# Routing products in another PSUM bank, and the last band's sums ahead of the maps' combination

## The reference

```python
x_proj = einsum('bchw,oc->bohw', x, proj_w)               # 128 -> 64 channels
att1 = _route(x_proj, att1_w, att1_b, [w3, w5], [b3, b5], 1)          # depthwise, 3x3 or 5x5
att2 = _route(att1, att2_w, att2_b, [w7, w9, w11], [b7, b9, b11], 3)  # depthwise, dilation 3
out = concatenate([att1, att2], axis=1)
att = concatenate([out.mean(1), out.max(1)], axis=1)      # two maps per sample
att = sigmoid(conv2d(att, sp_w, pad 3) + sp_b)            # 7x7, 2 -> 2
gate = att[:, 0:1] + att[:, 1:2]
return out * gate + x

def _route(x, att_w, att_b, conv_ws, conv_bs, dilation):
    pooled = x.mean(axis=(2, 3))
    idx = argmax(softmax(pooled @ att_w.T + att_b, axis=1), axis=1)   # which kernel this sample takes
    return the depthwise convolution of x with kernel idx
```

## Time and profile before

| | |
|---|---|
| median of three runs | 6009.83 us |
| profiled execution | 6016.42 us |
| span from first to last instruction in it | 6014.7 us |
| TensorE matmul busy | 4768.7 us (79%) |
| VectorE busy | 3136.8 us (52%) |
| ScalarE busy | 2827.8 us (47%) |
| GpSimd busy | 1039.5 us (17%) |
| DMA | mean 214 GB/s |

### The profile page before, as it was taken

One profiled execution on the slowest core, in us unless ns is written; L12 is line 12 of the kernel. 1 busy time (PEld: TensorE's weight loads), 2 busy tenths in 40 slices (PEclk: granted clock), 3 DMA queues, 4 the chain that ended last, 5 costly groups with the idle time before them and its releaser, 6 DMA issues.

```text
span 6014.7 us, 156600 instructions
## 1 busy us (share of the span) xinstructions
PE 4768.7 (79%) x62816; PEld 3244.4 (54%) x62816; DVE 3136.8 (52%) x3931; ACT 2827.8 (47%) x5378; POOL 1039.5 (17%) x1574
## 2 busy tenths in 40 slices
PE   5678887888878888887888888788888878885453
PEld 2336474655647465564746547474654747464453
DVE  3315455554645546474554547455464755545345
ACT  3455554544545454454545454454545445451120
POOL 2001011111112111121211111121111212111232
PEclk8889999988989989898999989899998989897675
DMA  9655787979888797988879788897978888796957
GB/s 241 185 159 172 173 209 226 230 219 224 237 210 218 216 233 218 222 244 209 218 219 235 216 222 244 200 227 213 237 219 222 246 202 224 211 213 176 221 135 198
DMA packets 1033176, 1284.58 MB, mean 214 GB/s; under 512 B 670749, under 2 KB 865736, under 8 KB 1001885
## 3 DMA queue, kind: packets, MB, share of 16 engines
q1 hardware_dynamic: 899468, 723.43, 50.5%
q0 software_dynamic: 64304, 410.01, 21.8%
q10 hardware_dynamic: 69026, 146.11, 9.5%
HBM read 950.16 MB, written 456.70 MB: 234 GB/s over the span
## 4 chain that ended last, share of the span: by engine, by line
PE 50%; DMA 21%; SPq 9%; DVE 8%; issue 7%; ACT 3%; ACTq 1%; POOL 1%; another core or an unknown queue 0%; DVEq 0%; POOLq 0%
PE psC L1086 19%; PE psA L1022 10%; PE psA L1023 9%; DMA RX<-w_d 6%; SPq L439 6%; DMA RX<-in_x_dram 5%; PE psB L1054 3%; PE psA L958 3%; PE psB L1065 2%; PE psB L1032 2%; DMA out_dram<-RX 2%; DMA RX<-nat_d 2%; DVE L L1375 2%; PE psB L967 2%; DMA map_d<-RX 2%
## 5 line engine op out<-in xcount | busy, mean ns | idle before, releaser
L1086 PE MATMUL psC<-RX 61*60 61x96 f32 (+7 forms) x49152 | 1479.9, 268 | 276.1 <-POOL RX L680 129.4
L1086 PEld LDWEIGHTS psC<-RX 61*60 61x60 f32 x49152 | 1412.8, 134 | 341.9 <-issue 329.2
L875 ACT ACTIVATE L<-psC 124x120 f32 (+4 forms) x2048 | 396.8, 287 | 885.6 <-PE psC L1086 830.5
L1022 PE MATMUL psA<-X,RX 128*128 128x240 f32 x1280 | 638.0, 588 | 129.7 <-ACT RX L840 128.2
L680 POOL COPY RX<-RX 64x720 f32<-64x720 f32 x512 | 426.2, 839 | 1408.8 <-DMA RX<-w_d 1407.5
L845 ACT ACTIVATE X<-psA,bias 128x246 f32<-128x246 f32 x1024 | 626.6, 722 | 56.2 <-issue 25.6
L1054 PE MATMUL psB<-ident,L 124*128 124x124 f32 x2160 | 381.1, 318 | 334.9 <-DVE RX L1395 163.7
L1310 DVE TENSOR_REDUCE MM<-L 124x135 f32<-124x2160 f32 (+1 forms) x192 | 535.3, 2844 | 212.7 <-ACT L L875 212.7
L1395 DVE TENSOR_TENSOR RX<-psB,RX 128x360 f32<-128x360 f32 (+7 forms) x1200 | 359.2, 350 | 546.5 <-PE psB L1054 485.6
L1023 PE MATMUL psA<-X,RX 128*128 128x240 f32 x1280 | 632.5, 583 | 0.0
L865 ACT ACTIVATE RX<-L 128x1080 f32 (+1 forms) x256 | 542.4, 2127 | 147.8 <-DMA L<-strip_d 147.7
(11 more groups left out here) (122 smaller groups left out, 5008.2 us busy)
## 6 DMA issues: line engine op xcount, KB each, us to landing
RX<-in_x_dram POOLq DMA_DIRECT2D x48, 2560.0 KB, 15.2
RX<-w_d ACTq DMA_DIRECT2D x512, 180.0 KB, 4.4
RX<-in_x_dram SPq DMA_DIRECT2D x128, 720.0 KB, 9.1
out_dram<-RX SPq DMA_DIRECT2D x128, 720.0 KB, 8.4
nat_d<-X SPq DMA_DIRECT2D x320, 280.0 KB
L<-strip_d SPq DMA_DIRECT2D x192, 405.0 KB, 10.5
strip_d<-nat_d SPq DMA_DIRECT2D x48, 1440.0 KB
RX<-nat_d POOLq DMA_DIRECT2D x130, 400.0 KB, 5.1
```

Of the source, the lines that this page charges most:

```text
L875: ins = nc.scalar.activation(dst[:, 0:NU2 - par, 15 * r:15 * r + nq, par, :], src[:, par:BR:2, :, :], ACT.Identity)
L1022: nc.tensor.matmul(o[:, :, 0:T1], w[:, ch, 96:224], rhs, start=True, stop=False, skip_group_check=True)
L1086: ins = nc.tensor.matmul(o[:, :, 0:kk, a:b], w2t[2 * q + p][rows, ch, z:z + PB], src[rows, 2 * p + ch, 0:nf, 3 * cg + dc:3 * cg + dc + kk, ...
```

## The change

The product of the sums (L1002) leaves `route` and becomes `route_stats`, which TensorE runs before the last fill's transposes. It and the three logits products write columns 400 to 451 of psC[3], which nothing else uses, in place of psA[0]; so the wait for ScalarE's last copy out of psA goes. VectorE reads them there. On VectorE, `combine` moves from before `take_x` of band 5 to behind `route_means` and stands ahead of `route_indices`.

```diff
                     if f == MAPS_AFTER and t.two:
                         turn_map2(t.m)
+                route_stats(s)
                 turn_x(s, *fills[-1])
+
+            def route_stats(s):
+                if isinstance(s, int) and s == 0:
+                    pe.wait_ge(psum_set, 1)
+                wait_alone(pe, stats_ready, s + 1)
+                nc.tensor.matmul(psC[3][0:C2, 400:425], projt[:, :], stats[:, :, :].rearrange("p r c -> p (r c)"),
+                                 start=True, stop=True).then_inc(stats_mm, 1)
 
             def route(t):
                 s = t.s
-                pe.wait_ge(stats_ready, s + 1)
-                wait_alone(pe, xc_ready, NFS * (s + 1))
-                nc.tensor.matmul(psA[0][0:C2, 0:25], projt[:, :], stats[:, :, :].rearrange("p r c -> p (r c)"),
-                                 start=True, stop=True).then_inc(stats_mm, 1)
                 if t.two:
                     wait_alone(pe, proj_evac, NFS * (s + 1))
                     spatial(t.m, 0)
                 wait_alone(pe, pool_ready, s + 1)
-                for n, (o, m, rhs) in enumerate(((32, 2, a1t), (40, 3, a2t), (48, 3, a2t))):
-                    ins = nc.tensor.matmul(psA[0][0:1, o:o + m], pooled[:, n:n + 1], rhs[:, :], start=True, stop=True)
+                for n, (o, m, rhs) in enumerate(((432, 2, a1t), (440, 3, a2t), (448, 3, a2t))):
+                    ins = nc.tensor.matmul(psC[3][0:1, o:o + m], pooled[:, n:n + 1], rhs[:, :], start=True, stop=True)
...
-                step(nc.vector.tensor_copy(psx[:, :, :].rearrange("p r c -> p (r c)"), psA[0][0:C2, 0:25]))
+                step(nc.vector.tensor_copy(psx[:, :, :].rearrange("p r c -> p (r c)"), psC[3][0:C2, 400:425]))
...
                     for b in range(2, NB1 - 1):
                         take_x(s, b)
-                if t.two:
-                    combine(m)
                 if t.new:
                     take_x(s, NB1 - 1)
                     stats_total(s)
                     route_means(s)
+                if t.two:
+                    combine(m)
+                if t.new:
                     route_indices(s)
```

More of the change, by code:

```diff
@@ L1255, in route_indices @@
                 dve.wait_ge(logits_mm, s + 1)
-                step(nc.vector.tensor_tensor(lg[:, 0:2], psA[0][0:1, 32:34], attb[:, 0:2], ALU.add))
-                step(nc.vector.tensor_tensor(lg[:, 2:5], psA[0][0:1, 40:43], attb[:, 2:5], ALU.add))
-                step(nc.vector.tensor_tensor(lg[:, 5:8], psA[0][0:1, 48:51], attb[:, 2:5], ALU.add))
+                step(nc.vector.tensor_tensor(lg[:, 0:2], psC[3][0:1, 432:434], attb[:, 0:2], ALU.add))
+                step(nc.vector.tensor_tensor(lg[:, 2:5], psC[3][0:1, 440:443], attb[:, 2:5], ALU.add))
+                step(nc.vector.tensor_tensor(lg[:, 5:8], psC[3][0:1, 448:451], attb[:, 2:5], ALU.add))
                 l2 = lg[:, 2:8].rearrange("p (v k) -> p v k", k=3)
```

## The result

The changed kernel took **6091.28 us** as the median of four runs (6084.23 to 6111.00) against 6000.84 us for the kernel before in the same session. The ratio is 1.0158, with a 95% interval of 1.0124 to 1.0191: 1.6% slower. Its profiled execution took 6084.23 us, of which 6082.5 us are the span; the forecast made against the profiled execution was 6083.5.

The account below looks back on a forecast made before the run. No engine bounds the kernel for long; each turn is a chain of hand-overs. 47.7 (order) + 20.2 (clock) - 0.8 = +67.1 us on the median 6009.83 gives 6077 us, 1.1% slower; range 6030 to 6105.

Parts of the forecast that it names:

- What sets the first convolution's start: Start of each turn: the two halves of the 7x7 convolution set the first convolution's start, not the routing.
- Rivals A: Absorbed: later in the turn, the later start costs nothing or only part; 6043 half absorbed, 6010 wholly; chance 0.14.
- B: Faster: the longer quiet stretch lets output-phase loads land sooner; 5999 with one load regained, 5920 with two; chance 0.06.
- Sums of band 5: VectorE, ahead of the maps: sums take 4.5 us from 2009.6, ready near 2014.1, 3.5 us before the product.
- Rival C: Ahead of the last transposes: sums are late and TensorE waits for them; 3 us in each turn gives 6119; chance 0.05.
- The combination behind the means: Before the 7x7 convolution: it can begin 5.42 us after the last transposes' end in each of 14 turns, +47.7 us.
- The clock: First half of the 7x7 convolution: longer wait loses 2.4 us of work per turn at half clock, +20.2 us.
- Rival D: 7x7 convolution: order only, the clock stays as it is; 6057; chance 0.13 together with partial clock cost.
- Turns 0 and 1: Turns without a combination, logits waiting for the means: gain up to 0.76 us each, counted as -0.8 us.
- the 14 gaps sum to 28.13 us: Baseline from last transposes to 7x7 convolution, a mean of 2.0 us, subtracted from 14 x 5.42.
- eight of them pay 1.69 us: Baseline of the 7x7 convolution's first halves: eight of 14 run partly at 1.2 GHz, 13.4 us in all.
- allowance of 15 us for hand-overs that come out longer: Up to 15 us added above the forecast's clock bounds of 6067 to 6085; chance 0.62 for that whole span.

Follow-up runs that it names:

- product-alone kernel: Changed kernel with VectorE's combination put back ahead of band 5's sums; the product's early place and new bank stay; ratio 1.0056 to the kernel before.

## Why the prediction was right, and where it was short

- **What sets the first convolution's start** was read rightly. In all profiles it begins 6.2 to 6.9 us behind the 7x7 convolution, and nothing absorbed a later start: gaps and halves grew by 77 us and the mean span by 81. The remainder got no shorter, which both absorption and regained loads would have made it. Rivals A and B are out.
- **Sums of band 5.** Expected to take 4.5 us from the landing and to be ready 3.5 us ahead of the product; measured 2029.87 to 2034.44 with the product at 2037.86, 3.4 us. TensorE waited for the sums ahead of the product in none of the 16 turns. Rival C is out.
- **The combination behind the means.** Expected 5.42 us per gap, measured 5.27 to 5.32: +46.1 us for the forecast's +47.7. The difference is the last transposes, which the product between them holds up by some 0.1 us.
- **The clock.** Expected +20.2 us on the profile, measured +22.0, sized by analogy with another wait of the same trace. Rival D is out, but that the size is so near is in part luck. The analogy took a longer wait for a dearer one, and behind gaps of 6.12 us the halves lost 2.2 us each, less than the 2.5 and 2.6 behind 5.31. And the 2.4 us of work that it took for lost ahead of the first convolution are for the most part not lost there: the first eight matmuls behind that wait take 3.3 to 3.4 us at either clock. The Trainium skill (TensorE: Matmul & The Clock Gate, HAM oscillation) says that waits between bursts of matmuls bring each burst back to half clock; here it held behind the 5.3 us, all 14 halves being slow (mean clocks of 0.55 to 0.65).
- **Turns 0 and 1.** The product came 0.9 us ahead of the last transposes' end in both, and the first convolution of turn 1 began 1.3 us sooner in the first profile and 0.8 us later in the second: the expected -0.8 us is lost in other variation, and no run shows it.
- **The term that was mis-sized** is the baseline. The step "the 14 gaps sum to 28.13 us" and "eight of them pay 1.69 us" took one execution for the kernel. In three profiles the gaps sum to 22.0 to 28.1 us and the halves to 57.7 to 69.4. With their means the forecast's own sum would have been 50.5 + 25.8 - 0.8 = +75.5 us, and the median 6085, not 6077.
- **What was luck.** The two profiled executions, 6083.5 forecast and 6084.23 measured, agree more closely than the kernels do: that of before lay above all timed runs of its session, that of after is the lowest of its four. By the medians the change was forecast at +67 us and measured at +90 (ratio 1.0158, in us 74 to 115). Of these 23 us, 9 are in the median of before, which a fourth run moved from 6009.83 to 6000.84, and 8 in the baseline above; the other 6 stay open. The range held the result by its allowance of 15 us for hand-overs that come out longer, and they did not: the gap was 5.31 us, not 5.42.

## What to carry to other kernels

Before removing a wait, ask who waits behind it and with how much slack; the long idle time here stood on an engine that was early. When an operation is moved down a list, put it where its engine is idle anyway (between the sums and the product), not behind a string of small dependent steps: one place decided between 1.5% slower and 0.2 to 0.4% faster. And where a term depends on the clock after a short wait, take it from several profiles, and see first whether the matmuls behind the wait run at the clock's pace at all.

## What the runs showed of the hardware that was not expected

- Whether TensorE falls to 1.2 GHz behind a gap of 0.9 to 2.9 us differs from one execution to the next: 8, 1 and 5 turns of 14 in three profiles of one kernel. All slow halves there stood behind gaps of 1.8 us or more, all fast ones behind 2.1 us or less; the gaps differ with the moment at which the maps land: in all 37 turns with a gap over 0.93 us, the 7x7 convolution begins 7.1 to 7.3 us behind the combination, which starts when they do. In the product-alone kernel the gap itself is 0.93 us, in one turn 1.10, and 8 of 14 halves are slow all the same. All eight stand in the ten turns in which TensorE also waited for the sums ahead of the four transposes, for 1.8 to 2.6 us; of these ten, one with a wait of 2.0 us and one with 0.9 were fast, as were all four without a wait. So four transposes between two waits did not keep the clock here.
- A longer wait did not cost more clock. Behind gaps of 5.31 us the halves took 91.4 and 92.8 us in 14 turns, behind 6.12 us 86.2, behind 7.02 us 85.5. Each of the last two comes from one profile.
- Filling matmuls that cover 4.3 of 5.3 us keep 2.4 GHz in all 14 turns; 12 of them in a wait of 6.2 us, which left TensorE idle for some 1.0 us ahead of the first convolution, did so in seven turns of 14.
- The first eight matmuls of the first convolution (240 columns, float32) take 3.38 us at a granted clock of 0.50 and 3.28 us at 1.00, while a half of the 7x7 convolution takes 4.00 us at 1.00 and 5.69 at 0.70.
